# MetaFormer block on one core: the gather and pair loops written out as straight code

## What is computed

```python
# block 1: deformable convolution of the channel-normalised image
o = conv3x3(ln_c(x), offset_w) + offset_b        # 18 offsets and 9 masks per pixel
for each of 9 taps:                              # py, px = base + offset
    v = bilinear(xT, py, px) * sigmoid(mask)     # 4 corner pixels, 128 channels each
x = x + einsum("bkhwc,ock->bohw", v, dcn_w)

# block 2: experts, routed by a graph attention layer
h = ln_t(t) @ W_gat                              # t: the tokens
e = leaky_relu(a_src[src] + a_dst[dst])          # 524288 edges and 4096 self loops
alpha = softmax of e over the edges of one dst
scores = layernorm(segment_sum(h[src] * alpha, dst) + b_gat)
w, experts = softmax(top_k(scores, 2))
t = t + sum over experts of w * (gelu(t' @ W1[e] + b1[e]) @ W2[e] + b2[e])
```

## Time and profile before

| | |
|---|---|
| three runs | 812.37, 815.66, 815.75 us, median 815.66 |
| profiled execution, span | 997.0 us (its time without the profile is not listed) |
| mean granted PE clock in it | 0.796 |
| busy | PE 682.4, DVE 539.3, POOL 521.8, ACT 439.0 us |
| indirect DMAs | 288 in the gather loop, 160 in the pair stage |

### The profile page before, as it was taken

One profiled execution on the slowest core, in us unless ns is written; L12 is line 12 of the kernel. 1 busy time (PEld: TensorE's weight loads), 2 busy tenths in 40 slices (PEclk: granted clock), 3 DMA queues, 4 the chain that ended last, 5 costly groups with the idle time before them and its releaser, 6 DMA issues.

```text
span 997.0 us, 13929 instructions
## 1 busy us (share of the span) xinstructions
PE 682.4 (68%) x4148; PEld 571.9 (57%) x4148; DVE 539.3 (54%) x2035; ACT 439.0 (44%) x1251; POOL 521.8 (52%) x543
## 2 busy tenths in 40 slices
PE   7836548548576877678777776973291991994986
PEld 5626547547466777667666766851160761672655
DVE  7648546445465565655656553960150550552887
ACT  4646256356266744667446644430120330330057
POOL 3074474474477766776667720057476276276003
PEclk7977688688689777898777867595596896896899
DMA  8982462362455446454464520100000000011002
GB/s 254 293 318 67 126 183 83 113 180 83 116 156 152 137 137 176 144 152 148 136 177 143 152 84 1 19 5 6 4 5 5 2 5 5 1 6 5 1 1 86
DMA packets 59844, 96.40 MB, mean 97 GB/s; under 512 B 20008, under 2 KB 39340, under 8 KB 59564
## 3 DMA queue, kind: packets, MB, share of 16 engines
q0 software_dynamic: 28160, 76.67, 27.4%
q1 hardware_dynamic: 31660, 19.44, 6.4%
HBM read 85.03 MB, written 11.01 MB: 96 GB/s over the span
## 4 chain that ended last, share of the span: by engine, by line
PE 30%; ACT 26%; another core or an unknown queue 23%; issue 11%; DVE 9%; DMA 0%; SPq 0%; DVEq 0%; ACTq 0%
ACT arena L761 21%; PE bank L621 8%; PE bank L554 6%; PE bank L611 4%; PE bank L530 3%; PE bank L602 3%; PE bank L508 3%; ACT scratch L768 2%; PE bank L538 1%; DVE x_all L1469 1%; ACT arena L867 1%; DVE pairs L1163 1%; DVE stats L1123 1%; DVE pairs L1162 1%
## 5 line engine op out<-in xcount | busy, mean ns | idle before, releaser
L410 POOL DMA_INDIRECT arena<-cells,idx_slot x288 | 312.3, 1085 | 86.6 <-issue 83.1
L761 ACT ACTIVATE arena<-arena,w_slot 128x128 f32<-128x128 f32 x896 | 273.0, 398 | 1.1 <-DMA arena<-cells,idx_slot 1.1
L530 PE MATMUL bank<-ident,arena 128*128 128x128 f32 x1152 | 172.2, 306 | 78.1 <-ACT arena L761 46.1
L554 PE MATMUL bank<-padded 128*64 128x64 bf16 x1024 | 136.6, 290 | 94.8 <-issue 94.8
L530 PEld LDWEIGHTS bank<-ident,arena 128*128 128x128 f32 x1152 | 147.8, 158 | 93.2 <-ACT arena L761 55.6
L554 PEld LDWEIGHTS bank<-padded 128*64 128x64 bf16 x1024 | 123.2, 203 | 107.4 <-issue 105.4
L768 ACT COPY scratch<-bank 128x384 f32<-128x384 f32 x97 | 45.7, 472 | 238.2 <-remote 130.4
L611 PE MATMUL bank<-w_sb,scratch 128*128 128x128 f32 x512 | 69.9, 294 | 77.7 <-ACT scratch L820 72.1
L611 PEld LDWEIGHTS bank<-w_sb,scratch 128*128 128x128 f32 x512 | 68.4, 209 | 88.9 <-DVE arena L1268 44.5
L820 ACT ACTIVATE scratch<-bank,b_sb 128x512 f32<-128x512 f32 x64 | 43.2, 687 | 163.1 <-PE bank L602 83.5
L621 PE MATMUL bank<-scratch,n_tok 128*128 128x320 f32 x320 | 98.0, 458 | 17.6 <-DVE scratch L1235 10.9
(11 more groups left out here) (238 smaller groups left out, 746.2 us busy)
## 6 DMA issues: line engine op xcount, KB each, us to landing
cells<-n_tok SPq DMA_DIRECT2D x16, 512.0 KB, 6.6
arena<-cells,idx_slot POOLq DMA_INDIRECT x288
arena<-in_L_ffn_edge_index_dram SPq DMA_DIRECT2D x2, 2048.0 KB
chan<-in_x_dram SPq DMA_DIRECT2D x4, 512.0 KB, 4.8
out_dram<-chan SPq DMA_DIRECT2D x8, 256.0 KB, 2.0
padded<-src_rows,src_idx POOLq DMA_INDIRECT x80
padded<-dst_rows,dst_idx POOLq DMA_INDIRECT x80
w_sb<-in_L_ffn_W_dram SPq DMA_DIRECT2D x2, 512.0 KB, 8.1
```

The costliest lines, as they stand in the source:

```text
L410: nc.gpsimd.indirect_dma_start(cell[:, u, k, :, :].rearrange("p c f -> p (c f)"), None, cells[:, :], bass.IndirectOffsetOnAxis(ap=idx_slot ...
L530: mm = nc.tensor.matmul(banks[g][:, j * P:(j + 1) * P], cell[:, u, 3 * g + j, c, :], ident[:, :], is_transpose=True, start=(c == 0), stop= ...
L554: mm = nc.tensor.matmul(hist, onehots[:, 0, :, c], onehots[:, 1, :, c], start=False, stop=False)
L761: ins = nc.scalar.activation(cell[:, u, k, c, :], cell[:, u, k, c, :], ACT.Copy, scale=w_slot[:, u, c, k:k + 1])
```

## The change

All loops of the gather part and the pair stage are written out in Python, on POOL, PE, ACT and DVE. Every wait is now on a constant and sits on the instruction that needs it. The gates are gone: 48 (L407) and 8 (L423) on POOL, 272 (L1030) on DVE. Indices are made as integers (`idx_i`, `pk_src`, and row 2 of `pk_i`) and read where they lie by the DMAs, weights are read from `corner_w`, so that the 96 + 4 copies to `idx_slot`, the 32 to `w_slot` and 20 of `src_idx` and `dst_idx` go, and with them DVE's waits for ACT in `weights`. POOL's group n now waits for its own slot alone (`turned`, group n - 6), and once per image for `sampled`. In the pair stage the copies are replaced by one tiny copy that signals `pair_used`. Four memsets at the start go. PE gets a wait `conv_read` on a residual that its order covered before.

```diff
-            with pool.Fori(0, NT // 2) as it:
-                for u in range(2):
-                    for g in range(3):
-                        n = 6 * it + 3 * u + g
-                        if (3 * u + g) % 2 == 0:
-
-                            pool.wait_ge(idx_ready, n + 2)
-                            pool.wait_ge(turned, n + 2)
-                            pool.wait_ge(gate_done, 3 * it + (3 * u + g) // 2 + 1)
-                            nc.gpsimd.tensor_tensor(pool_gate[:, 0:1], ident[:, 0:1], ident[:, 1:2], ALU.add)\
-                                .then_inc(gate_done, 1)
...
+            for t in range(NT):
+                u = t % 2
+                if t % TB == 0:
+                    pool.wait_ge(sampled, t // TB + 1)
+                for g in range(3):
+                    if t >= 2:
+                        pool.wait_ge(turned, 3 * (t - 2) + g + 1)
+                    for k in range(3 * g, 3 * g + 3):
+                        nc.gpsimd.indirect_dma_start(
+                            cell[:, u, k, :, :].rearrange("p c f -> p (c f)"), None, cells[:, :],
+                            bass.IndirectOffsetOnAxis(ap=idx_i[:, t, k:k + 1], axis=0))\
+                            .then_inc(cells_in[3 * u + g], 16)
...
-                    pool.wait_ge(pair_idx_ready, 2 * it + u + 1)
-                    pool.wait_ge(gate_done, 2 * it + u + 1 + 3 * NT // 2)
-                    nc.gpsimd.tensor_tensor(pool_gate[:, 2 + u:3 + u], ident[:, 0:1], ident[:, 1:2], ALU.add).then_inc(gate_done, 1)
...
+                if p >= 2:
+                    pool.wait_ge(pair_used, p - 1)
...
-            with pe.Fori(0, NT // 2) as it:
...
+            for m in range(3 * NT):
+                turn(m)
+                if m > 0:
+                    weigh(m - 1)
+                if m % 6 == 5:
+                    pe.wait_ge(hot_ready, m // 6 + 1)
...
-                def weights(u):
-
-                    ve.wait_ge(scaled_a, 6 * it + 3 * u + 3)
-                    ve.wait_ge(scaled_v, 6 * it + 3 * u + 3)
...
                     top = kept[:, 8 * rnd:8 * rnd + 8]
-                    take_wait()
                     st.add(V.max(top, ka))
-                    corner_tap(0, rnd)
+                    corner_tap(2 * it, rnd)
                     ve.wait_ge(dve, st.now())
                     if rnd < CAP // 8:
-                        take_wait()
-                        st.add(V.match_replace(ka, top, ka, 0.0))
-                        if rnd % 3 == 0:
-                            next_indices(0, rnd)
-                        ve.wait_ge(dve, st.now())
+                        done(V.match_replace(ka, top, ka, 0.0))
...
-                for idx, pk in ((src_idx, pk_src), (dst_idx, pk_dst)):
-                    ins = V.tensor_scalar(idx[:, u, :], pk[:, bass.ds((s + 2) * SUB, SUB)], 0.0, None, ALU.add)
-                ins.then_inc(pair_idx_ready, 1)
+                V.tensor_copy(act_gate[:, 1:2], ident[:, 0:1]).then_inc(pair_used, 1)
```

More of the change, by code:

```diff
@@ L268, in metaformer @@
         dve = sem("dve")
-        idx_ready = sem("idx_ready")
+        sampled = sem("sampled")
         cells_in = [sem(f"cells_in{s}") for s in range(6)]
-        scaled_a, scaled_v, w_ready, turned, samp_ready, conv_done = (
-            sem(n) for n in ("scaled_a", "scaled_v", "w_ready", "turned", "samp_ready", "conv_done"))
+        scaled_a, scaled_v, turned, samp_ready, conv_done, conv_read = (
+            sem(n) for n in ("scaled_a", "scaled_v", "turned", "samp_ready", "conv_done", "conv_read"))
         hot_ready, hist_done = sem("hot_ready"), sem("hist_done")
@@ L638, in pair_step @@
                     down(p + 2, e)
-            with pe.Fori(0, NSUB // 2 - 2) as it:
-                pair_step(2 * it, 0)
-                pair_step(2 * it + 1, 1)
-            pair_step(NSUB - 4, 0)
+            for p in range(NSUB - 3):
+                pair_step(p, p % 2)
             for p in range(NSUB - 3, NSUB):
@@ L761, in scale, with evict @@
                         ins = nc.scalar.activation(cell[:, u, k, c, :], cell[:, u, k, c, :], ACT.Copy,
-                                                   scale=w_slot[:, u, c, k:k + 1])
+                                                   scale=corner_w[:, t, c, k:k + 1])
                 ins.then_inc(scaled_a, 1)
-            def evict(n, u, g):
-                ac.wait_ge(turned, n + SLOTS)
-                nc.scalar.copy(samp[:, u, 3 * g:3 * g + 3, :], banks[g][:, 0:3 * P]).then_inc(samp_ready, 1)
-            with ac.Fori(0, NT // 2) as it:
-                for u in range(2):
-                    n = 6 * it + 3 * u
-                    scale(it, u, 0)
-                    evict(n, 1 - u, 2)
-                    scale(it, u, 1)
-                    evict(n + 1, u, 0)
-                    scale(it, u, 2)
-                    evict(n + 2, u, 1)
-            evict(3 * NT, 1, 2)
+            def evict(m):
+                t, g = divmod(m, 3)
+                ac.wait_ge(turned, m + 1)
+                nc.scalar.copy(samp[:, t % 2, 3 * g:3 * g + 3, :], banks[g][:, 0:3 * P]).then_inc(samp_ready, 1)
+            for m in range(3 * NT):
+                scale(m)
+                if m > 0:
+                    evict(m - 1)
+            evict(3 * NT - 1)
             ac.wait_ge(cells_out[B - 1], 64)
@@ L838, in _ @@
             pair_step(-1, 2)
-            with ac.Fori(0, NSUB // 2 - 2) as it:
-                pair_step(2 * it, 1)
-                pair_step(2 * it + 1, 1)
-            pair_step(NSUB - 4, 1)
+            for p in range(NSUB - 3):
+                pair_step(p, 1)
             pair_exp(NSUB - 2)
@@ L993, in sampling @@
                 done(ins)
+                V.tensor_copy(act_gate[:, 2:3], ident[:, 0:1]).then_inc(sampled, 1)
             ve.wait_ge(w_in, 16 * len(PARAMS))
@@ L1318, in _ @@
             unpack(OWN, PC)
-            loop_at = st.now()
-            with ve.Fori(0, NSUB // 2 - 2) as it:
-                st.base, st.n = it * 2 * PAIR_STEPS + loop_at, 0
-                pair_step(2 * it, it, 0)
-                pair_step(2 * it + 1, it + 1, 1)
-                assert st.n == 2 * PAIR_STEPS, st.n
-            st.base, st.n = loop_at + 2 * PAIR_STEPS * (NSUB // 2 - 2), 0
-            pair_step(NSUB - 4, NSUB // 2 - 2, 0)
+            for p in range(NSUB - 3):
+                pair_step(p, p % 2)
             for p in (NSUB - 3, NSUB - 2):
```

216 lines of the change are left out of this document (83 added, 133 removed).

## The result

The changed kernel takes 792.72 us (median of 4 runs, 791.76 to 799.26), the kernel before 814.43 (4 runs, 812.37 to 815.75): ratio 0.9752, 95% interval 0.9718 to 0.9786. It is 21.7 us faster, 17.4 to 23.0 by the interval; 16.1 were forecast, to 799.6.

The account below looks back on a forecast made before the run. POOL's list of DMAs was taken to bound the gather loop and, by a hair, the pair stage. Gains of 4.0 + 4.2 + 7.5 + 0.4 = 16.1 us off 815.66 gave 799.6 us, range 784 to 826.

Parts of the forecast that it names:

- POOL as the bound: Gather loop: POOL's list of DMAs sets the pace at 26.1 us an iteration, PE and ACT in turn need 25.1.
- Part 1: Gather loop: 45 POOL gates behind the start go, each costing 0.09 us with nothing hiding it; 4.0 us gained.
- Part 2: Start of the gather loop: POOL's 19th DMA waits for one slot instead of two; 4.2 us gained.
- Part 3: Way into the pair stage: POOL's change of code between all-reduce and gate goes, first pair data come sooner; 7.5 us gained.
- Part 4: Pair stage: 7 POOL gates of 0.06 us each go; 0.4 us gained, with POOL as the bound.
- Part 5: DVE: 272 gates and some 150 copies go, hidden by DVE's 6 us of slack to POOL an iteration; 0 gained.
- Part 6: Register work on ACT and PE, branches, four memsets, added tiny signals and the `conv_read` wait: 0 beside running work.
- I take these pauses for the recording's: Whole profile: engines' unexplained standstills, about 181 us of the span, taken as absent from plain runs; only distances outside them read.
- rival B: No change: DMAs pay the change of code, PE and ACT set the gather loop; 812 to 815 us, chance 0.12.
- Rival C: Slower: the longer straight code needs some 65 instruction fetches, holding engines 1.45 us each; 830 us, chance 0.12.
- Rival D: More: DMAs held up less than gates, or pauses partly loop work; up to 25.3 us for gates, 778, chance 0.11.
- Rival A: Only a part: DMAs pay the change of code (807.1 us) or PE and ACT set the gather loop (803.6); chance 0.15.

## Why the prediction was right, and where it wasn't

- **POOL as the bound**: right, also in its size. It was put together from single rows of a disturbed execution: 26.1 us an iteration. In the kernel with the loops written out it is 394.3 / 15 = 26.3. The slack to the chain of PE and ACT was given as 1.0 us an iteration; with the hold-up taken away PE's histograms follow each other every 24.95 us, against the 25.1 that were added up. POOL's own distances (369.7 / 15 = 24.6) say less about the chain, since POOL starts with six free slots and so runs ahead of it.
- **Part 1, POOL's gates, 4.0 us**: 6.4 by the traces with the loops written out and after (394.3 to 387.9 from the 19th DMA on), 1.6 by the trace with the gates put back, 5.5 by its time. Right in kind, the size uncertain; that the hold-up beside the one-hots moves to the DMAs and stays was right (50 us).
- **Part 2, the start, 4.2 us**: the 19th DMA starts at 76.62 and at 72.69, 3.9 us. Right in size. But POOL didn't wait for the first turn any more, which had ended at 69.3, 3 us before its 18th DMA. With the loops written out alone the first turn ended at 73.2, so the second slot cost 3.4 us there; the rest of the 3.9 is luck: DVE's start of the loop lies between 61.0 and 66.0 us in the traces without pauses, and was late in that one.
- **Part 3, the change of POOL's code, 7.5 us**: the distance fell by 8.6 us, 14.8 to 6.2. Right as a sum, wrong in its reason. The prediction gave all of it to the gate that goes away; 7.1 belong to the loop's branch, which kept the change of code behind the wait for the rows, and 1.5 to the gate. It had the change of code as what "only the gate made necessary"; that holds, but with the gate in straight code nothing measurable is lost. That the sum came out is luck of a kind: gate and branch went in the same edit. What this term is worth in time was not measured alone.
- **Part 4**, 0.4 us, is too small to be seen. **Part 5**, DVE's gates and copies at 0: right for the gates; the copies were not put back alone. DVE's busy time fell by 29 us (539.3 to 510.1), not by the 45 that were named as a sign.
- **Part 6, branches and register work at 0**: open. The loops alone were worth 10.5 us, and 7.1 of them are explained by distances; the other 3 or so are no more than the interval, and no run took them apart. The same holds for the 5.6 us by which the whole forecast was short (21.7 measured, 16.1 forecast): 1.1 is in part 3, up to 2.4 in part 1, the rest unexplained. Some of it may be no effect at all: 792.72 is the median of four executions, and the kernels with one gate and with DVE's gates, which should cost 1.5 us or nothing, took 795.
- **The pauses**: the step "I take these pauses for the recording's" was wrong. Executions without a profile take as long in the sets that have them, and the changed kernel pauses there just as well. The forecast survived because only distances outside the pauses went into it, and by luck, because the executions of the result had none. With pauses rival B, no change, is what happened: there POOL waits 118 us for PE, so that what is saved on POOL can be waited away.
- **Rival C**, instruction fetches: 62 packets where 65 were estimated, and histogram matmuls in straight code that waited 0.0 us. No cost of them shows. **Rival D** didn't come: the hold-up is there after the change, 1.123 us a DMA. **Rival A** didn't come either: the DMAs follow the landing without a change of code, and the chain stays 0.7 us below POOL's pace.

On the two pages of the Trainium skill: the 6.9 us of a change of code in three traces (6.94, 6.98, 6.87) lie 1 us above the about 6 us that "GPSIMD Engine Reference", section Instruction dispatch, gives for the first call into freshly loaded code. That the gap is this load is argued from its size and its place. DMAs don't need it (723.28 follows 722.29 directly in the kernel after). "SBUF — State Buffer", section Who interferes with whom, was half right: two inputs from SBUF are what blocks (0.953 against 1.123 us a DMA), but they block the DMAs too, and the page supposed that the making of descriptors wouldn't be blocked.

## What to carry to other kernels

An operation of another kind on GpSimd brought a change of code of 7 us in this kernel. In straight code it ran beside the wait ahead of it (7.7 us from the all-reduce to the first DMA). Behind a loop's branch, which took over that wait, it came after it (14.8 us). Put one such operation ahead of the branch, or use none at all. When the engine that bounds a stage is held up by a neighbour, take away the hold-up and the chain that lies 1 us behind it at once: alone the one brought 4 to 7 us here, both together 42 to 45.

## What was not expected of the hardware

- In some sets of executions the same program takes 990 us instead of 793, profiled or not, with matmuls behind pauses of 1.1 us that wait for nothing, at a mean granted clock of 0.792 instead of 0.864. One chip had sets of both kinds.
- The comparison of 1024 bf16 numbers with one input from PSUM takes 0.680 us and nearly keeps the pace of two inputs from SBUF (4096 results in 2.5 us for 2.28), and doesn't hold GpSimd's DMAs.
- With the histogram spread out, PE's granted clock in the gather loop was 1.00, for 0.85 after the change: after the change the turn behind the histogram runs at the lower of the two levels, 1.2 GHz (granted clock 0.50, 2.82 us), right behind 64 small products in one piece; behind 16 of them the turns stay at 2.4 GHz (1.00) and take 1.53. How much of the 42 us is the clock and how much the opened chain wasn't taken apart.
